# Head-softmax attention: the last addition over the heads moves from GpSimd to two matmuls in PSUM

## What is computed

```
scores = jnp.einsum('bhqd,bhkd->bhqk', mh_q, mh_k) / sqrt(HD)
score = jax.nn.softmax(scores, axis=1)
att = jnp.einsum('bhqk,bhkd->bhqd', score, mh_v)
```

## Time and profile before

| | us |
|---|---|
| median of 3 runs | 2386.59 (2386.57 to 2392.28) |
| profiled execution | 2385.77 |
| its span | 2383.9 |
| TensorE busy | 1849.6 (78%) |
| VectorE busy | 1479.6 (62%) |
| ScalarE busy | 1065.9 (45%) |
| GpSimd busy | 845.6 (35%) |

### The profile page before, as it was taken

The page is one execution under the profiler, slowest core; times in us unless marked ns, Lnnn a source line. Parts: engine busy times, 40 slices in busy tenths (PEclk is TensorE's granted clock), DMA queues, the critical chain, the costliest instruction groups (busy, mean ns, idle before and its releaser), DMA issues. The chain is left out here.

```text
span 2383.9 us, 32207 instructions
## 1 busy us (share of the span) xinstructions
PE 1849.6 (78%) x11358; PEld 932.5 (39%) x11381; DVE 1479.6 (62%) x2569; ACT 1065.9 (45%) x1794; POOL 845.6 (35%) x763
## 2 busy tenths in 40 slices
PE   5787979999874767766856888999767868999844
PEld 3345423333452444434743652333245435222223
DVE  3444256663765999983343558999435454877486
ACT  2353124544333444541442433888713343366636
POOL 1000025554245999993021042666532213000012
PEclk9898989999987898896977999999868888699967
DMA  5611461110038023003218335221232104533000
GB/s 167 162 38 40 160 218 62 62 45 1 18 112 171 15 41 63 1 2 136 85 60 239 81 119 142 59 59 39 106 119 88 51 1 147 130 73 58 10 0 18
DMA packets 172242, 190.65 MB, mean 80 GB/s; under 512 B 14708, under 2 KB 138686, under 8 KB 171046
## 3 DMA queue, kind: packets, MB, share of 16 engines
q1 hardware_dynamic: 169012, 180.20, 27.8%
q0 software_dynamic: 3072, 8.39, 1.1%
HBM read 124.17 MB, written 68.30 MB: 81 GB/s over the span
## 5 line engine op out<-in xcount | busy, mean ns | idle before, releaser
L3163 POOL TENSOR_TENSOR a2x_masked<-a2x_masked,tall_rows 128x512 f32<-128x512 f32 x128 | 163.3, 1276 | 110.9 <-ACT a2x_masked L3125 110.9
L1374 ACT ACTIVATE experts<-a1x_scores 128x1024 f32<-128x1024 f32 x128 | 124.1, 1021 | 154.7 <-PE a1x_scores L1305 154.7
L3174 DVE TENSOR_REDUCE a3x_row_most<-a3x_ring 128x1 f32<-128x512 f32 x256 | 159.3, 682 | 41.4 <-PE a3x_ring L3021 41.4
L3174 DVE TENSOR_REDUCE a2x_row_most<-a2x_ring 128x1 f32<-128x512 f32 x256 | 162.1, 679 | 3.0 <-remote 1.9
L1411 POOL TENSOR_TENSOR a1x_tree<-experts 128x1024 f32<-128x1024 f32 x64 | 150.4, 2350 | 33.0 <-ACT experts L1374 32.8
L656 POOL TENSOR_TENSOR a0x_pair_sums<-a0x_probs_T 128x1024 f32<-128x1024 f32 x48 | 114.7, 2390 | 129.3 <-ACT a0x_probs_T L785 101.9
L839 DVE TENSOR_REDUCE ctx_then_heads<-a0x_rows 128x2 f32<-128x1024 f32 x88 | 107.7, 1224 | 81.8 <-PE a0x_rows L674 81.6
L1343 DVE TENSOR_TENSOR experts<-experts,a1x_inverse_total 128x2048 f32<-128x2048 f32 x64 | 145.7, 2276 | 4.5 <-ACT a1x_inverse_total L1387 4.5
L3118 ACT ACTIVATE a3x_probs_T<-a3x_scores_T 128x1024 f32<-128x1024 f32 x128 | 123.3, 1018 | 49.4 <-PE a3x_scores_T L3048 49.3
L1294 PE MATMUL a1x_scores<-a1x_qs,a1x_ks 96*128 96x128 bf16 x1024 | 91.5, 242 | 62.8 <-ACT experts L1374 45.1
L3118 ACT ACTIVATE wide_rows<-a2x_masked 128x1024 f32<-128x1024 f32 x128 | 135.9, 1062 | 1.4 <-POOL a2x_masked L3163 1.4
(11 more groups left out here) (651 smaller groups left out, 4275.5 us busy)
## 6 DMA issues: line engine op xcount, KB each, us to landing
v_scr<-p0x_vout SPq DMA_DIRECT2D x24, 256.0 KB, 2.0
k_scr<-p0x_x SPq DMA_DIRECT2D x24, 256.0 KB, 2.3
ctx_then_heads<-k_scr SPq DMA_DIRECT2D x8, 768.0 KB
a0x_vs<-v_scr SPq DMA_DIRECT2D x8, 768.0 KB, 4.7
experts<-in_L_ffn_w SPq DMA_DIRECT2D x8, 768.0 KB, 6.5
v_scr<-experts SPq DMA_DIRECT2D x16, 256.0 KB, 2.2
a1x_vs<-v_scr SPq DMA_DIRECT2D x16, 256.0 KB, 5.7
v_scr<-p2x_vout SPq DMA_DIRECT2D x16, 256.0 KB, 2.4
```

The lines of the kernel that those rows point to most:

```text
L1374: nc.scalar.activation(ex[:, n % E, 8 * half:8 * half + 8, :], sp_[:, g % 3, :, :, :].rearrange("p i j q -> p (i j) q"), ACT.Exp).then_inc ...
L3163: nc.gpsimd.tensor_tensor(sm[:, i % 2, 1, :], sm[:, i % 2, 1, :], full[1][:, i // 2 % KT, :], ALU.add).then_inc(pool_masked, 1)
L3174: nc.vector.tensor_reduce(rm[:, u % 2, h * QT + qt:h * QT + qt + 1, part], ring[:, row_place(r) % 3, 0:n], AX.X, ALU.max).then_inc(row_mos ...
```

## The change

GpSimd stops at two sums for each tile, in one tile of two buffers. TensorE gets `add_up(m)`: two fp32 matmuls with the identity as weights, which add the two sums in PSUM, in the second quarter of rp, the tile whose first quarter holds the inverse. It waits for the two sums and for the divide of m-1, since both engines would use the same bank. ScalarE's logarithm reads that quarter. GpSimd waits for `total` before it overwrites a buffer of two sums.

```diff
-        tree3 = st.sb("tree3", [P, 2, P])
-        tot = st.sb("total", [P, 2, P])
+        tree3 = st.sb("tree3", [P, 2, 2, P])
...
+                def add_up(n):
+                    pe.wait_ge(two_sums, n + 1)
+                    if n:
+                        pe.wait_ge(normed, n)
+                    for h in range(2):
+                        mm = nc.tensor.matmul(rp[:, 1, :], core.ident[:, :], tree3[:, n % 2, h, :], start=(h == 0),
+                                              stop=(h == 1))
+                    mm.then_inc(total, 1)
+
...
                 for n in range(N):
                     if n + 1 < N:
                         score(n + 1, 0)
+                    if n >= 2:
+                        add_up(n - 2)
                     shift(n)
                     if n + 1 < N:
                         score(n + 1, 1)
                     if n >= 2:
                         value(n - 2)
+                add_up(N - 2)
+                add_up(N - 1)
                 value(N - 2)
                 value(N - 1)
...
-                    nc.scalar.activation(logs[:, :], tot[:, n % 2, :], ACT.Ln).then_inc(logged, 1)
+                    nc.scalar.activation(logs[:, :], rp[:, 1, :], ACT.Ln).then_inc(logged, 1)
...
-                    pool.wait_ge(folded, n * 3 + 1)
+                    pool.wait_ge(folded, n * 2 + 1)
                     nc.gpsimd.tensor_tensor(tree2[:, :, :], tree[:, 0:4], tree[:, 4:8], ALU.add).then_inc(folded, 1)
-                    pool.wait_ge(folded, n * 3 + 2)
-                    nc.gpsimd.tensor_tensor(tree3[:, :, :], tree2[:, 0:2], tree2[:, 2:4], ALU.add).then_inc(folded, 1)
-                    pool.wait_ge(folded, n * 3 + 3)
+                    pool.wait_ge(folded, n * 2 + 2)
                     if n >= 2:
-                        pool.wait_ge(logged, n - 1)
-                    nc.gpsimd.tensor_tensor(tot[:, n % 2], tree3[:, 0], tree3[:, 1], ALU.add).then_inc(total, 1)
+                        pool.wait_ge(total, n - 1)
+                    nc.gpsimd.tensor_tensor(tree3[:, n % 2], tree2[:, 0:2], tree2[:, 2:4], ALU.add).then_inc(two_sums, 1)
```

More of the change, by code:

```diff
@@ L1220, in head_softmax_stage @@
         minus_in = st.sem("minus_in")
-        scored, most_half, most, less, expd, folded, total = (
-            st.sem(x) for x in ("scored", "most_half", "most", "less", "expd", "folded", "total"))
+        scored, most_half, most, less, expd, folded, two_sums, total = (
+            st.sem(x) for x in ("scored", "most_half", "most", "less", "expd", "folded", "two_sums", "total"))
         logged, inverse, normed = st.sem("logged"), st.sem("inverse"), st.sem("normed")
```

## The result

The changed kernel takes 2416.18 us (median of 4 runs, 2412.41 to 2417.08), before 2386.58 beside it: ratio 1.0119, 95% interval 1.0096 to 1.0142. It is slower by 30 us. 2407 was predicted, within 2389 to 2422.

What follows compares the result with a forecast made beforehand. VectorE's loop, with the joined halves in every third tile, was taken to set the pace. Tiles going from 5.15 to 5.51 us gave +22, copies -2, low clock +1: +21, so 2407 us, range 2389 to 2422.

Steps and rivals of the forecast that it cites:

- The closed loop: Divide, value, score, pair, logarithm, exponential, next divide: one tile long, 5.29 us, where the plain tile took 4.79.
- the plain tile: Attention tile whose maximum does not come in two halves: 4.79 us before, forecast no shorter than 5.29.
- The join: VectorE's L1359, joining the maximum's two halves in every third tile: median 0.60 us before, forecast near 1.3.
- the falls of the clock: Stretches of TensorE at 1.2 GHz, a fifth of the stage before; the forecast has none left.
- the held join: L1359 held by GpSimd's L1413 on the shared SBUF port, making its tile 5.82 us.
- the forecast has no such stretches left: Low-clock stretches after a shift that waited for L1359; said to vanish because the pair fills TensorE's longest pause.
- The rival of the falling clock: TensorE's clock keeps falling in the stage, about ten tiles' time: +13 us, 2420 us; chance 0.17.
- the collision: GpSimd's L1413 begins 0.18 us before VectorE's L1359 and holds it; tile 5.82 us.
- the signs of being wrong: Pair well under 0.6 us, VectorE not waiting for ScalarE, or the stage's 345 us not becoming about 366.
- D: Start of a tile's divide on VectorE; L1359 was put at D + 4.66, L1413 at D + 4.48.
- The case without the collision: L1413 comes after L1359's start, all tiles take 5.29 us: +8, 2395 us; chance 0.16.
- The faster rival: Inverse not late, through a short pair or TensorE reaching it earlier: -9 to -14 us, about 2377; chance 0.09.

Runs made afterwards that it cites:

- the kernel of both edits: Changed kernel with the pair one tile earlier in TensorE's order, ahead of value, and the halves joined by a one-SBUF-input reduce: 2374.3 us, ratio 0.9940 to before.
- the early pair: Changed kernel with the pair one tile earlier in TensorE's order, ahead of the value step: 2375.4 us, ratio 0.9947 to before.
- the filled kernel: Changed kernel with sixteen score matmuls repeated behind the pair, ahead of the shift, in every third tile: 2402.7 us, ratio 1.0066 to before.
- three additions, filled: Kernel before without GpSimd's fourth addition, with eight score matmuls repeated ahead of each shift: 2384.6 us, ratio 0.9987 to before.
- four additions and the fill: Kernel before with 16 more score matmuls ahead of the shift in every third tile: 2387.2 us, ratio 0.9996 to before.
- join as a reduce: Changed kernel with the halves of the maximum joined by a reduce with one SBUF input: 2389.6 us, ratio 1.0010 to before.
- three additions filled more: Kernel before without GpSimd's fourth addition, eight score matmuls repeated ahead of each shift, two half tiles in every third tile: 2374.2 us, ratio 0.9938 to before.
- the pair twice: Changed kernel with the pair computed twice in place, four matmuls for two: 2422.5 us, ratio 1.0146 to before.
- Relief of GpSimd alone: Kernel before with GpSimd's fourth addition left out and nothing put in its place: 2385.5 us, ratio 0.9982 to before.

## Why the prediction was right, and where it was off

The direction and the forecast's chain of causes held. The inverse is late because the pair stands behind value and score; moving it alone undoes that. The closed loop sets the plain tile; doubling the pair adds 0.44 us to it. The join collides with GpSimd's second addition, and a join with one SBUF input escapes. What the forecast left out is a third part, the falls of the clock.

The 28 us of the stage divide by the runs into 12.5 for falls of the clock (373.3 to 360.8), 15.7 for the held join (360.8 to 345.1, two runs with the clock at 1.00 and the same loop), and nothing for the loop by itself (345.1 to 345.2). This nothing is a balance: the loop costs 12.3 us (332.8 to 345.1), and a relieved GpSimd with a clock that stays up, as in the kernel of both edits, gives about as much back (345.2 to 332.8). The parts are not independent: without the loop the divide doesn't wait, and without that wait GpSimd's second addition begins behind the join, by 0.33 us with the early pair.

What was off:

- The step that failed is the sentence "the forecast has no such stretches left, since the pair fills TensorE's longest pause". It doesn't. The held join makes the pause ahead of the shift 1.36 to 1.56 us even behind the pair, and the clock fell there. With falls 2416 was measured, without 2403. The rival of the falling clock had a chance of 0.17 and a price of 13 us; the measured price is 12.5. It even names the pause of some 1.4 us that a held join leaves, but the forecast itself, given 0.50, took the collision into its sum and the pause as filled. So the rival is what happened, and 2416 lies within the range because the range reached up to it. Of the signs of being wrong one came: the stage became 373 us, not about 366.
- The tiles without falls were forecast at 5.82, 5.43 and 5.29, mean 5.51. They are 5.90, 5.26 and 5.14, mean 5.43, and the filled kernel has 5.41. That is 5 us too much over the stage, and by luck it hid part of the missing 12.5. The loop was 0.15 too long: 0.09 from score to pair, 0.04 from pair to logarithm, and 0.03 of the logarithm, which is 277 ns with its operand in PSUM where it was 310.
- The collision held by luck too. Its margin was put at 0.18 us and shrinks with the shorter loop to 0.03 (D - 0.65 + 5.28 = D + 4.63 against D + 4.66); 0.02 or 0.03 was measured in 11 of the 21 joins, 0.11 or 0.12 in 7.
- The case without the collision was put at +8. The run has +2, with an interval that includes no change, since the loop is shorter (5.14 for 5.29).
- The faster rival was put down to a short pair. It takes a pair in another place; its size, -9 to -14, was right (-12).

The Trainium skill's rule on the port (SBUF — State Buffer, Who interferes with whom) is that whoever starts first keeps it. One direction of it shows here: each join that was held met an addition that had started first, by only 0.02 us in the tile above, and ended 0.15 us behind it. With the early pair GpSimd's first addition is over 0.25 us after the join starts, and the join takes 0.40. The other direction, a join that starts first and holds GpSimd, stands in no trace here.

## What to carry to other kernels

Where work moves to an engine with time to spare, ask what stands ahead of it in that engine's order: two matmuls of 0.66 us cost nothing ahead of the value step and closed a loop behind it, which with all that followed made 40 us. Follow each new wait one step further, to what it does to the pauses of the engine whose clock depends on them; a fill of repeated matmuls is a cheap test of that. And where a join of two SBUF tiles beside a busy GpSimd is held for long, a reduce is worth trying, which here takes 423 ns in every case: it took 28 us off the stage of the changed kernel, 4 off that of the kernel before and less than 1 with the early pair.

## What the runs showed of the hardware

- TensorE's clock fell behind pairs of pauses of 0.86 and 0.74 us (three additions, filled) and of 1.46 and 0.74 us (changed), and not behind each of them. With four additions and the fill no pause from 770 to 1050 us is longer than 0.85, and it still fell (0.96). Where the pauses ahead of the shift were 0.7 us or less (changed and filled, early pair, join as a reduce, three additions filled more) it stayed at 1.00, though a single pause elsewhere in the loop reached 1.10. And with the pair twice, where up to 0.88 us lie ahead of the shift and 0.85 ahead of value, it fell only twice. What decides was not settled. The Trainium skill (TensorE: Matmul & The Clock Gate, A second HAM failure mode) names short idle times between groups of matmuls as a cause. The trace agrees, with the pauses of 0.86 and 0.74 us above.
- Relief of GpSimd alone took 2.7 us off the stage (345.2 to 342.5), a fill alone 1.1 (to 344.1, clock 0.96), relief and a fill that keeps the clock at 1.00 together 12.5 (to 332.7).
